# Keeping the transposed tokens of a token-mixing and mixture-of-experts kernel in memory, and taking them back without TensorE

## The reference

```python
xn = (x - mean(x)) / sqrt(var(x) + 1e-5)
# branch 1: a linear recurrence over the tokens of a sequence, gated
q, v = xn @ Wq, xn @ Wv
state[t] = sigmoid(beta) * state[t-1] + v[t]
y = layernorm(q * state) * ln_g + ln_b
branch1 = (y * silu(xn @ Wg)) @ Wo
# branch 2: a mixture of experts, at most 128 tokens for each
w, idx = top_k(softmax(xn @ router_w.T), 8); w = w / sum(w)
for each expert e and its tokens:
    h = silu(xn_e @ w1[e].T) * (xn_e @ v1[e].T)
    branch2[tokens] += w * (h @ w2[e])
out = x + branch1 + branch2
```

## Time and profile before

| | before |
|---|---|
| timed runs, median (lowest to highest) | 2571.91 us (2571.17 to 2572.86) |
| the profiled execution's own time | 2574.14 us |
| its span, first to last instruction | 2572.4 us |
| PE (TensorE matmuls) busy | 2517.9 us, 98% |
| VectorE (DVE) busy | 1639.7 us, 64% |
| ScalarE (ACT) busy | 1294.4 us, 50% |
| GpSimd (POOL) busy | 670.3 us, 26% |
| mean granted TensorE clock | 0.993 |
| HBM read and written | 520.89 MB and 85.50 MB |

### The profile page before, as it was taken

How to read it: one execution, slowest core, us unless ns; L and a number is a source line. 1 busy time by engine, 2 the same in 40 slices (tenths; PEclk the granted TensorE clock), 3 DMA queues, 4 the chain that set the end, 5 groups by cost and what they waited for, 6 DMA issues and landing times.

```text
span 2572.4 us, 39705 instructions
## 1 busy us (share of the span) xinstructions
PE 2517.9 (98%) x13849; PEld 2234.3 (87%) x13849; DVE 1639.7 (64%) x1725; ACT 1294.4 (50%) x1471; POOL 670.3 (26%) x523
## 2 busy tenths in 40 slices
PE   7999999899999999999999999999999999999997
PEld 6888977898889988899888898888988889988897
DVE  6776798656566665666566656656665565666654
ACT  4445323555446644556445554545654456545554
POOL 2121022223322222222223222322222232322321
PEclk9999999999999999999999999999999999999999
DMA  6663754796567966679766697666986668866686
GB/s 241 225 219 119 219 194 148 244 309 219 196 211 252 298 218 226 217 230 290 246 225 201 211 311 256 215 215 200 285 278 196 225 220 270 267 228 224 190 272 172
DMA packets 147614, 590.54 MB, mean 230 GB/s; under 512 B 20128, under 2 KB 36576, under 8 KB 147040
## 3 DMA queue, kind: packets, MB, share of 16 engines
q1 hardware_dynamic: 112128, 503.71, 54.7%
q0 software_dynamic: 35424, 86.00, 16.1%
HBM read 520.89 MB, written 85.50 MB: 236 GB/s over the span
## 4 chain that ended last, share of the span: by engine, by line
PE 89%; DVE 7%; ACT 1%; issue 1%; DMA 1%; POOL 0%; DVEq 0%; ACTq 0%; POOLq 0%
PE psA L1489 17%; PE psA L1491 17%; PE psA L1490 17%; PE psH L1489 7%; PE psH L1491 6%; PE psH L1490 6%; PE psY L1489 4%; PE psY L1491 3%; PE psY L1490 3%; PE psX L1595 2%; PE psY L1520 2%; DVE top L1092 1%; DVE keys L1098 1%; PE psH L1656 1%; PE psX L1615 1%
## 5 line engine op out<-in xcount | busy, mean ns | idle before, releaser
L1108 DVE TENSOR_TENSOR ew_lo<-ew_raw,ew_hi 128x1536 fp32r<-128x1536 f32 x384 | 693.6, 1816 | 345.0 <-ACT ew_hi L725 330.6
L725 ACT ACTIVATE ew_hi<-ew_raw 128x1536 fp32r<-128x1536 f32 x384 | 568.4, 1484 | 153.9 <-DMA ew_raw<-ew_dram 113.1
L1489 PE MATMUL psA<-xT_hi,pw_hi 128*128 128x512 f32 x1536 | 620.3, 404 | 9.5 <-DVE xT_lo L1023 4.8
L719 ACT ACTIVATE pw_hi<-pw_raw 128x1024 fp32r<-128x1024 f32 x254 | 266.0, 1059 | 687.7 <-PE psA L1491 683.8
L1491 PE MATMUL psA<-xT_hi,pw_lo 128*128 128x512 f32 x1536 | 609.5, 397 | 0.0
L1490 PE MATMUL psA<-xT_lo,pw_hi 128*128 128x512 f32 x1536 | 605.4, 394 | 0.0
L1103 DVE TENSOR_TENSOR pw_lo<-pw_raw,pw_hi 128x1024 fp32r<-128x1024 f32 x256 | 312.3, 1230 | 172.1 <-ACT pw_hi L719 165.8
L1489 PE MATMUL psH<-ew_hi,gT_hi 128*128 128x384 f32 x1024 | 353.3, 345 | 7.7 <-DVE ew_lo L1108 7.0
L1489 PEld LDWEIGHTS psA<-xT_hi,pw_hi 128*128 128x128 f32 x1536 | 290.0, 189 | 72.3 <-issue 5.7
L1491 PEld LDWEIGHTS psA<-xT_hi,pw_lo 128*128 128x128 f32 x1536 | 290.9, 189 | 70.1
L1490 PEld LDWEIGHTS psA<-xT_lo,pw_hi 128*128 128x128 f32 x1536 | 293.6, 191 | 63.8
(11 more groups left out here) (164 smaller groups left out, 3368.3 us busy)
## 6 DMA issues: line engine op xcount, KB each, us to landing
ew_raw<-ew_dram SPq DMA_DIRECT2D x384, 768.0 KB, 6.5
pw_raw<-proj_w_dram SPq DMA_DIRECT2D x256, 512.0 KB, 4.9
xn_scratch<-xt SPq DMA_DIRECT2D x33, 512.0 KB, 4.2
xt<-x_dram SPq DMA_DIRECT2D x32, 512.0 KB, 5.5
out_dram<-x_dram SPq DMA_DIRECT2D x32, 512.0 KB, 6.1
out_dram<-ot POOLq DMA_DIRECT2D x32, 512.0 KB, 13.1
xn<-xn_scratch SPq DMA_DIRECT2D x29, 512.0 KB, 5.7
xn_scratch<-wt SPq DMA_DIRECT2D x33, 32.0 KB, 3.3
```

The lines of the kernel that those rows point to most:

```text
L719: act.activation(dst[:, slot, :, :], pw_raw[:, slot, :, :], ACT.Copy).then_inc(s_pwhi, 1)
L725: act.activation(ew_hi[:, c % 3, :], ew_raw[:, c % 3, :], ACT.Copy).then_inc(s_ewhi, 1)
L1108: dve.tensor_tensor(ew_lo[:, c % 3, :], ew_raw[:, c % 3, :], ew_hi[:, c % 3, :].bitcast(F32), ALU.subtract).then_inc(s_ewlo, 1)
L1489: pe.matmul(dst, l_hi, r_hi_, start=first, stop=False)
```

## The change

Tiles 4 to 31 are kept after their first transposition. In block 0 ScalarE copies the transposed tile from its PSUM bank once more, as it is, to a new buffer `xraw` (two of them, in the place of `ot`), SP stores it to a new scratch `xn_turned`, and the low half is subtracted from `xraw` instead of from the bank. In the output rounds SP loads a tile from `xn_turned`, and both halves are made from it; TensorE's second transposition is gone. SP's next load of such a tile now waits until the low half has been made.

```diff
@@ SP
             def router_step(k):
+                if k > NT:
+                    wait_alone(sp, s_praw, k - NT)
+                    sp.dma_start(turned[k - 1, :, :], xraw[:, (k - 1) % 2, :, :].rearrange("p k c -> p (k c)")
+                                 ).then_inc(s_tst[(k - 1) % 2], 16)
                 if k + 1 < NTILE:
                     wait_alone(sp, s_xn, k + 2)
...
-            def load_xn(row):
-                sp.dma_start(xn[:, :], scratch[bass.ds(row, P), 0:D]).then_inc(s_xnl, 16)
+            def load_xn(tile):
+                sp.dma_start(xn[:, :, :].rearrange("p k c -> p (k c)"),
+                             turned[bass.ds(tile, 1), :, :].rearrange("a p c -> p (a c)")).then_inc(s_xnl, 16)
...
             def next_xn(j, mm):
-                sp.wait_ge(s_xT, 4 * j + mm + 1)
-                load_xn((j + 1) * TB + (mm + 1) * P)
+                sp.wait_ge(s_xlo, 4 * j + mm + 1)
+                load_xn((j + 1) * NT + mm + 1)
...
             router_step(NTILE)
+            sp.dma_start(turned[NTILE, :, :], xt[:, 7, :]).then_inc(s_spare, 16)
...
+            for u in range(2):
+                sp.wait_ge(s_tst[u], 16 * (NTILE - NT) // 2)
-            load_xn(TB)
+            load_xn(NT)
@@ ScalarE
             def turned_hi(k):
                 act.wait_ge(s_pT, k + 1)
                 dst = xT_hi[:, :, k * P:(k + 1) * P] if k < NT else rt_hi[:, k % 2, :, :]
+                if k >= NT:
+                    if k >= NT + 2:
+                        wait_alone(act, s_tst[k % 2], 16 * ((k - NT) // 2))
+                    act.activation(xraw[:, k % 2, :, :], chunks(bank_of(k)), ACT.Copy).then_inc(s_praw, 1)
                 act.activation(dst, chunks(bank_of(k)), ACT.Copy).then_inc(s_phi, 1)
...
             def take_xT(j, mm):
-                act.wait_ge(s_xT, 4 * j + mm + 1)
-                act.activation(xT_hi[:, :, bass.ds(mm * P, P)], chunks(psH), ACT.Copy).then_inc(s_xhi, 1)
+                act.wait_ge(s_xnl, 16 * (4 * j + mm + 1))
+                act.activation(xT_hi[:, :, bass.ds(mm * P, P)], xn[:, :, :], ACT.Copy).then_inc(s_xhi, 1)
 
             for u in range(4):
                 act.wait_ge(s_xst[u], 16 * (NTILE // 8))
+            for u in range(2):
+                act.wait_ge(s_tst[u], 16 * (NTILE - NT) // 2)
@@ VectorE
-                dve.tensor_tensor(dst, chunks(bank_of(k)), hi.bitcast(F32), ALU.subtract).then_inc(s_plo, 1)
+                raw = chunks(bank_of(k)) if k < NT else xraw[:, k % 2, :, :]
+                dve.tensor_tensor(dst, raw, hi.bitcast(F32), ALU.subtract).then_inc(s_plo, 1)
...
-                dve.tensor_tensor(xT_lo[:, :, c], chunks(psH), xT_hi[:, :, c].bitcast(F32),
+                dve.tensor_tensor(xT_lo[:, :, c], xn[:, :, :], xT_hi[:, :, c].bitcast(F32),
@@ TensorE
                 if k >= NTILE - KC:
-                    pe.wait_ge(s_plo, k)
+                    pe.wait_ge(s_phi, k)
+                    pe.wait_ge(s_plo, k - 1)
...
-                if mm > 0:
-                    pe.wait_ge(s_xlo, mm)
-                xn_turn(0, mm)
...
-            xn_turn(1, 0)
...
-            pe.wait_ge(s_xlo, 5)
...
-            xn_turn(1, 1)
...
-            pe.wait_ge(s_xlo, 6)
...
                 hidden_turn(e)
-                if not last:
-                    xn_turn(j, mm)
```

More of the change, by code:

```diff
@@ L124, in build @@
         ln6T = place("ln6T", [P, KC, P], F32R)
-        xn = place("xn", [P, D], F32)
+        xn = place("xn", [P, KC, P], F32)
+        at_o = top[0]
         ot = place("ot", [P, 2 * NT, 2 * P], F32)
+        xraw = place("xraw", [P, 2, KC, P], F32, at_o)
         at_e = top[0]
@@ L184, in build @@
         scratch = nc.dram_tensor("xn_scratch", (NTOK + P, XW), F32).ap()
+        turned = nc.dram_tensor("xn_turned", (NTOK // P + 1, P, D), F32).ap()
         unused = nc.dram_tensor("unused", (2, P, 4), F32).ap()
@@ L204, in build @@
         s_pT = sem("s_pT")
+        s_praw = sem("s_praw")
+        s_tst = [sem(f"s_tst{u}") for u in range(2)]
         s_phi, s_plo = sem("s_phi"), sem("s_plo")
@@ L245, in build @@
         s_xnl = sem("s_xnl")
-        s_xT = sem("s_xT")
         s_xhi, s_xlo = sem("s_xhi"), sem("s_xlo")
@@ L456, in _ @@
                     sp.wait_ge(s_wst, 16 * NTILE)
-                    sp.wait_ge(s_spare, 32)
+                    sp.wait_ge(s_spare, 48)
                     for c in range(3):
@@ L635, in _ @@
                         pool.wait_ge(s_xst[u], 16 * (NTILE // 8))
-                    pool.wait_ge(s_spare, 32)
+                    pool.wait_ge(s_spare, 48)
                     gather(0)
@@ L1651, in shift @@
                           ).then_inc(s_sh, 1)
[L1653 to L1658, removed]
             for k in range(NT):
```

## The result

The changed kernel takes 2563.04 us (median of 7 runs, 2560.12 to 2565.18), the one before 2572.63 us (7 runs): ratio 0.9962, 95% interval 0.9951 to 0.9973. It is faster by 9.6 us where 20.4 were predicted, and lies above the range. Its profiled execution took 2563.26 us.

What follows compares the result with a forecast made beforehand. TensorE was taken as the bound, busy 98% of the span; costs of 4.0 us minus a gross gain of 24.6 gave -20.6 net, 2553.5 us profiled and 2551.5 us as timed median, range 2546.5 to 2557.5.

Steps and rivals of the forecast that it cites:

- gross of 24.6 us: All blocks: total gain from removing 28 second transpositions, 17.6 + 1.8 + 0.2 + 0 + 5.0 us.
- the 20 full rounds: Blocks 2 to 6: 20 removed turns on a full TensorE at 0.88 us each, 17.6 us gained.
- block 1's rounds 2 and 3: Same order of work as blocks 2 to 6: two turns at 0.88 us, 1.8 us gained.
- block 0's rounds: Four turns, 3.5 us on TensorE, plus 1.5 us of VectorE lateness: 5.0 us gained, lower end 3.5.
- VectorE's debt: After block 0's rounds VectorE starts the first scan 1.5 us late, passed on through pw_lo waits; predicted to go.
- filler: Block 1, round 1: TensorE waits for hT_lo even without the turn, so 0 gained; round 0 was put at 0.2 us.
- Costs 1 and 2: Block 0, tile 8 and first gate projection: low halves of tiles 6 and 23 start one copy later, +0.95 us each.
- Cost 3: End of gate part: tile 31's low half starts later and queues with POOL's z_lo and wt, +1.0 us (0.5 to 1.8).
- Rival B: Low halves blocked by POOL's SBUF port use at tiles 6, 23 and 31: 3.4 us more, 2555 us, chance 0.08.
- Cost 4: Block 0: tiles 12, 17 and 22 may hold ScalarE up to 1.5 us for a store, +0.3 us (0 to 2).
- rival D: Stores block ScalarE at four tiles inside projections, costing 4 x (L - 5) us; 2579 us at L = 12; chance 0.03.
- Cost 5: Longer waits at tile 8 and first gate projection may add or lengthen a lower-clock stretch, +0.8 us (0 to 3.4).

Runs made afterwards that it cites:

- Gain alone: Changed kernel without raw copies, stores and their waits, low half read from PSUM, output rounds loading untransposed rows and not turning them: 2549.00 us, ratio 0.9905 to before.
- costs alone: Changed kernel's block 0 kept, but output rounds load the untransposed tile and turn it on TensorE as before: 2586.53 us, ratio 1.0055 to before.
- early stores: Changed kernel with each raw tile's store issued at the end of its own router step instead of the start of the next: 2555.59 us, ratio 0.9938 to before.
- no stores: Changed kernel without the 28 stores and the waits for them, copies kept, output rounds loading untransposed rows: 2558.11 us, ratio 0.9939 to before.
- three buffers: Changed kernel with three raw tiles in SBUF instead of two, stores still issued late: 2553.96 us, ratio 0.9927 to before.
- low half from PSUM: Changed kernel with stores issued at the end of the tile's own step, and low half read from PSUM behind the copy: 2556.52 us, ratio 0.9937 to before.

## Why the prediction missed

**The gross of 24.6 us was right.** Gain alone measured 23.7. In the trace of the changed kernel TensorE is 5.4 us later than before at the start of block 2 and 11.8 us earlier in block 7 (2467.72 against 2479.48), so the 20 full rounds gave 17.2 us; block 1's rounds 2 and 3 gave 1.8 as predicted; and block 0's rounds gave 5.0, since the scan after them is released by TensorE:

```profile
325.35 1.28 DVE L1157 TENSOR_TENSOR_SCAN st<-lam,start,psA 128x512 f32<-128x512 f32 x1 [0.37 <-PE psA L1511]
```

When these rounds begin, with the longer stretch at the lower clock behind it, TensorE is 12.9 us later than before; at this scan it is 7.8 (317.54 before). VectorE's debt is gone, and with it one of four `pw_lo` waits. At block 1's round 1 the transposition was filler, as argued (1.17 us for hT_lo); the first two rounds together gave some 0.6 us for the 0.2 forecast.

**Costs 1 and 2** (tile 8, first gate projection) measured 0.94 and 1.21 us for 0.95 each. **Cost 3** (1.0) measured 0.40 + 0.76 = 1.2 us, by the mechanism named. VectorE and POOL at the end of the changed kernel's gate part:

```profile
262.93 1.23 DVE L1043 TENSOR_TENSOR rt_lo<-xraw,rt_hi 128x1024 fp32r<-128x1024 f32 x1 [0.43 <-ACT rt_hi L712]
264.07 1.49 DVE L1077 TENSOR_TENSOR wt<-ex,mk 128x256 f32<-128x256 f32 x1
...
263.49 1.79 POOL L604 TENSOR_TENSOR z_lo<-yb,z_hi 128x512 fp32r<-128x512 f32 x1 [5.76 <-ACT z_hi L791]
```

`z_lo` begins inside the low half and takes 0.53 us longer than its 1.26, near the 0.67 us from its start to the low half's end; `wt`, 0.40 us when alone, ends just behind it. That is the exclusive lock of the Trainium skill's page SBUF — State Buffer, section Who interferes with whom, and the trace agrees. With the low half read from PSUM `z_lo` took 1.26 us again. Rival B, the same at two more places, did not occur.

**Cost 4 is the step that failed first**: "tiles 12, 17 and 22 may hold ScalarE for up to 1.5 us; tile 12 has over a microsecond of room before TensorE notices", +0.3 us. The place, the order in SP's list and the buffer were right. The size was not. The store was issued 1.2 us later than I had it (94.71 for 93.5), but the need came a microsecond later too, so that is not what failed. What failed is the landing: 6.2 us where I had put 4.0, the median of 25 stores in the earlier trace rows. Two of those 25 token stores took 6.1 and 6.7 us in the kernel before already (issued at 135.46 and 141.50), so the slow ones were there to be seen; and with the new stores the medians rose. The DMA issues of the changed kernel, 60 to 260 us:

```profile
xn_turned<-xraw SPq DMA_DIRECT2D x24, 512.0 KB, 5.1
xn_scratch<-xt SPq DMA_DIRECT2D x24, 512.0 KB, 4.7
```

From issue to need there were 4.0 us, which the median just met, and 1 us of room behind that; I priced it as if every store took the median. With 6.2 us ScalarE is held 2.4 us longer than by TensorE, the tile's room is used up, and the next tile's `xt` is late. The second piece was in no term: VectorE's low half and `keys` come late too, which costs TensorE 1.29 us. Cost measured: 4.2 us for 0.3. It is rival D's mechanism, a store that blocks ScalarE, with L (its time to landing) at some 6 us. D's formula gives 4 x (6.2 - 5) = 4.8 us, but that this is near 4.2 is in part luck: it counts four tiles, and only two (12 and 17) cost nearly all, one of them through `keys`.

**Cost 5 (clock, +0.8)** was too small as well: 3.4 us behind the new waits at 104 and 106, about 1 us at z's last slice. I read the first as a consequence of cost 4, since it stands right behind its waits; no experiment shows it apart from them. Its upper end, 3.4, was one stretch; there was that one and more.

The sum, between the two profiled executions (2574.14 and 2563.26 us, 10.9 gained, 9.7 fewer than the 20.6 of my net): cost 4 is 3.9 over, cost 5 3.6, costs 1 to 3 0.4, the full rounds 0.4. Another 0.9 us in block 0 has no wait to its name. Part of it is that a wait costs a little more than its listed length: at tile 8 the wait grew by 0.94 us and TensorE starts 1.07 us later (66.71 for 65.64), and there are eight such places. The last 80 us of the run lost 1.0, and block 1's first two rounds gave 0.4 more than I had. That makes 9.8. The bounds that I gave for the costs, 1.9 to 8 us, don't follow from my terms, whose ends add up to 2.4 and 9.1; with 9.1 the forecast would be 2556.4, still far below 2563.0. Of the medians, 10.8 us are missing, since I took the median to lie 2.2 us below the profiled execution, and for the changed kernel it lies 0.2 below.

## What to carry to other kernels

A buffer that is handed back by a DMA has a deadline: where the time from issue to need is near the median landing, count the landings above the median, allow for what the change adds to the queue, and look for what stands ahead of the issue in the queue's list. A new copy that no compute engine waits for belongs behind the work that somebody waits for; moving it there, with the low half back on PSUM, gave some 15 us here (2563.0 to 2548.1), more than the change itself had brought. And it pays to measure a change in two halves, gain alone and costs alone: they added up to 0.2 us and said at once which half of the sum was wrong.

## What was not expected of the hardware

TensorE's lower level (1.2 of 2.4 GHz, a granted clock of 0.50) came, up to the last rounds of a run, in stretches that lost about 1.7, 3.4 or 5.2 us of full clock. The same wait of 2.3 us at tile 8 was followed by one (early stores and no stores: 0.76 over 62 to 76 us) or not (the changed kernel, three buffers: 1.00). In the two kernels where it was, the first stretch had been short (0.83 over 20 to 30 us instead of 0.66). So the length of a wait alone did not decide it. Nor does the kernel alone: with the low half from PSUM one run took 2552.98 us at a mean granted clock of 0.994, and another 2559.60 us at 0.990. Each trace shows one execution, and where its stretches lie may be different in the next.
